# Folding the bias of the values into a bias row added in PSUM, and moving two pieces of VectorE's work to ScalarE, in a gated cross-attention with a mixture of experts

## The reference

```python
def attention(query, key, value, adj, mask):      # query = layernorm(x), key = value = ctx
    Q, K, V = heads(query @ Wq.T + bq), heads(key @ Wk.T + bk), heads(value @ Wv.T + bv)
    scores = Q @ K.T / sqrt(D) + adj              # per head, -inf where mask == 0
    out = merge(softmax(scores) @ V)
    return out @ Wo.T + bo

x = x + tanh(g_xattn) * attention(layernorm(x), ctx, ctx, adj, mask)
h = layernorm(x)
p = softmax(h @ gate_w.T);  e = argmax(p)         # one expert for each token
x = x + tanh(g_ffn) * p[e] * (relu(h @ w1[e] + b1[e]) @ w2[e] + b2[e])
```

## Time and profile before

| | us |
|---|---|
| three runs | 549.14, 551.38, 551.83 |
| median | 551.38 |
| span of the profiled execution, first to last instruction | 548.5 |
| PE busy in that span | 526.3 |
| DVE, ACT, POOL busy | 302.3, 309.1, 297.9 |

### The profile page before, as it was taken

The page is one execution under the profiler, slowest core; times in us unless marked ns, Lnnn a source line. Parts: engine busy times, 40 slices in busy tenths (PEclk is TensorE's granted clock), DMA queues, the critical chain, the costliest instruction groups (busy, mean ns, idle before and its releaser), DMA issues. The chain is left out here.

```text
span 548.5 us, 13306 instructions
## 1 busy us (share of the span) xinstructions
PE 526.3 (96%) x4123; PEld 405.1 (74%) x4124; DVE 302.3 (55%) x923; ACT 309.1 (56%) x678; POOL 297.9 (54%) x424
## 2 busy tenths in 40 slices
PE   8999999989999999999999999888999999999997
PEld 5577667667666667666676666658899999999996
DVE  2776587976677887668885878845340211111111
ACT  4366678665678665778675676664332333333322
POOL 5346566665567575468574556555244444443451
PEclk9999999999999999999999999999999999999999
DMA  8633625400405510204520057499136665555570
GB/s 288 206 110 132 192 65 183 149 31 6 150 21 192 166 50 1 79 10 153 180 85 1 11 184 250 147 362 320 59 103 218 211 205 196 178 187 184 189 210 1
DMA packets 51489, 77.67 MB, mean 142 GB/s; under 512 B 9945, under 2 KB 34601, under 8 KB 51305
## 3 DMA queue, kind: packets, MB, share of 16 engines
q1 hardware_dynamic: 46600, 67.72, 37.0%
q0 software_dynamic: 4192, 8.73, 5.0%
q10 hardware_dynamic: 640, 0.52, 0.3%
HBM read 52.76 MB, written 8.35 MB: 111 GB/s over the span
## 5 line engine op out<-in xcount | busy, mean ns | idle before, releaser
L1588 DVE CUSTOM_DVE_ANT_0 prob<-bank,adjm 128x512 f32<-128x512 f32 x256 | 172.3, 688 | 70.6 <-issue 39.9
L1229 ACT ACTIVATE pt<-bank 128x512 f32<-128x512 f32 x256 | 152.1, 596 | 87.7 <-PE bank L951 81.2
L682 POOL TENSOR_SCALAR prob<-prob,negmax 128x512 f32<-128x512 f32 x190 | 132.0, 698 | 117.6 <-DVE negmax L1588 113.4
L951 PE MATMUL bank<-ident,prob 128*128 128x128 f32 x1024 | 154.8, 274 | 2.2 <-POOL prob L682 1.3
L951 PEld LDWEIGHTS bank<-ident,prob 128*128 128x128 f32 x1024 | 124.2, 141 | 39.7 <-issue 13.7
L1299 ACT ACTIVATE adjm<-bank,colsm 128x128 f32<-128x128 f32 x184 | 52.6, 368 | 105.0 <-PE bank L1127 80.0
L940 PE MATMUL bank<-w2s 128*128 128x512 bf16 x256 | 97.5, 381 | 8.5 <-DVE negmax L1588 5.7
L963 PE MATMUL bank<-pt,vals 128*32 128x256 f32 x1024 | 68.3, 385 | 0.9 <-DVE vals L1386 0.5
L1127 PEld LDWEIGHTS bank<-xT,pt 128*128 128x128 f32 x576 | 67.1, 192 | 0.9
L1127 PE MATMUL bank<-xT,pt 128*128 128x128 f32 x576 | 67.2, 275 | 0.0
L1137 PE MATMUL bank<-w2s,adjm 128*128 x288 | 65.1, 379 | 0.0
(11 more groups left out here) (195 smaller groups left out, 624.4 us busy)
## 6 DMA issues: line engine op xcount, KB each, us to landing
pt<-in_L_ffn_w SPq DMA_DIRECT2D x19, 1024.0 KB
w2s<-parts SPq DMA_DIRECT2D x96, 128.0 KB
w2s<-in_L_ffn_w SPq DMA_DIRECT2D x8, 1024.0 KB
maski<-in_mask_Bx1xSxS_ik SPq DMA_DIRECT2D x4, 1024.0 KB, 5.6
w2s<-parts SPq DMA_DIRECT2D x56, 64.0 KB, 2.1
xres<-in_x SPq DMA_DIRECT2D x18, 128.0 KB
x_d<-rows SPq DMA_DIRECT2D x18, 128.0 KB
xn_d<-rows SPq DMA_DIRECT2D x18, 128.0 KB
```

The costliest lines, as they stand in the source:

```text
L682: po.tensor_scalar(prob[:, m], prob[:, m], -1.0, negmax[:, m:m + 1], ALU.mult, ALU.add).then_inc(s_shpool, 1)
L951: mm = pe.transpose(tr_bank[n % NTB][:, c * P:(c + 1) * P], prob[:, n % TILES % NB, c * P:(c + 1) * P], ident[:])
L1229: act.activation(pt[:, g % 2, :, j, q2 * P:(q2 + 1) * P], tr_bank[c % NTB][:].rearrange("p (c q) -> p c q", c=QT), ACT.Exp).then_inc(s_cac ...
L1588: ve.tensor_tensor_reduce(out=prob[:, m % NB], in0=sc_bank[m % NS][:], in1=adjm[:, qt], scale=-1.0, scalar=BIG, op0=ALU.add, op1=ALU.min, ...
```

## The change

1. **Values.** `bvb` is no longer added. ACT evicts a half of the values in one instruction of 128 x 512, in the step in which DVE had evicted it. DVE does nothing for it.
2. **Bias row.** In the setup PE transposes `bv` (step 4), ACT evicts it, PE multiplies it with Wo (step 8), and DVE adds `bob` and splits the sum into three bfloat16 rows that lie in partitions 0, 32 and 64 of `bias3` (`join_bias`, seven instructions). POOL fills `pick`, a 128 x 128 bfloat16 matrix with ones in rows 0, 32 and 64. The gate's weights are transposed one step later than before.
3. **Output.** Each `out` use starts with one more matmul, `pick` x `bias3`, which puts the bias into PSUM. DVE's L1416 goes, and L1418 reads PSUM. Its bank is set free one step later, at the head of `row_stats`.
4. **Normalised row.** DVE's L1447 goes. ACT writes the row in two instructions, mean minus x, then times 1 / sigma, in the same steps `ROW_STEPS`, behind the evictions of the step and ahead of L1255; the second waits for the first. The row has the other sign, and the two evictions of transposed rows (L1201 for `x2T`, L1293 for `xgT`) multiply by -1.
5. **Behind batch 3** ACT writes both rows behind the second slot's hidden layer, ahead of the eviction of the third slot's rows.

```diff
...
     PRO = ["Wq", "Wk", "small", "next x", "next x", "next ctx", "next ctx", "next q", "next k", "next q", "next k",
-           "Wv", "Wo", "gate"]
+           "Wv", "bv", "Wo", "bias", "gate"]
...
     MASK_STEPS, LATE_MASK_STEPS = {42: 0, 44: 1}, {13: 2, 15: 3}
-    WV_STEP, WO_STEP, GATE_STEP, FIRST_NORM_STEPS = 3, 6, 8, (2, 3, 4, 5)
+    WV_STEP, BV_STEP, WO_STEP, BIAS_STEP, GATE_STEP, FIRST_NORM_STEPS = 3, 4, 6, 8, 9, (2, 3, 4, 5)
...
         bob = sb("bob", [P, E])
+        bias3 = sb("bias3", [P, E], BF16)
+        pick = sb("pick", [P, P], BF16)
...
         x2T = sb("x2T", [P, 2, EC, P])
+        bvT = x2T[:, 0]
...
         t_x, t_out = ([sem(f"{n}{k}") for k in range(2)] for n in ("t_xres", "t_out"))
+        s_bias, t_centred, s_centred = sem("bias"), sem("t_centred"), sem("centred")
...
             po.memset(logit[:], 0.0).then_inc(t_ones, 1)
+            po.memset(pick[:], 0.0).then_inc(t_ones, 1)
+            po.wait_ge(t_ones, 3)
+            for r in range(3):
+                po.memset(pick[32 * r:32 * r + 1], 1.0).then_inc(t_ones, 1)
...
                     pe.wait_ge(t_atT, b * 4 + k + 1)
+                    if b == 0 and k == 0:
+                        pe.wait_ge(s_bias, 7)
+                        pe.wait_ge(t_ones, 6)
                     o = bank_free(b, i)
+                    pe.matmul(o[:, 0:E], pick[:], bias3[:], start=True, stop=False)
                     for c in range(EC):
-                        mm = pe.matmul(o[:, 0:E], atT[:, u, c], wT[:, 3, c], start=c == 0, stop=c == EC - 1)
+                        mm = pe.matmul(o[:, 0:E], atT[:, u, c], wT[:, 3, c], start=False, stop=c == EC - 1)
...
                     turn_w(2, setup_at("Wv"))
+                if n == BV_STEP:
+                    pe.wait_ge(s_bcast, 64)
+                    o = bank_free(0, setup_at("bv"))
+                    for c in range(EC):
+                        mm = pe.transpose(o[:, c * P:(c + 1) * P], bvb[:, c * P:(c + 1) * P], ident[:])
+                    mm.then_inc(s_m, 1)
...
                     turn_w(3, setup_at("Wo"))
+                if n == BIAS_STEP:
+                    for w in ("bv", "Wo"):
+                        pe.wait_ge(s_md[setup_at(w) % 2], free(0, setup_at(w)) + 1)
+                    o = bank_free(0, setup_at("bias"))
+                    for c in range(EC):
+                        mm = pe.matmul(o[:, 0:E], bvT[:, c], wT[:, 3, c], start=c == 0, stop=c == EC - 1)
+                    mm.then_inc(s_m, 1)
...
+            def values(b, i, h):
+                act.wait_ge(s_m, ready(b, i))
+                if b == 0 and h == 0:
+                    act.wait_ge(s_vinit, 2)
+                act.activation(vals[:, 2 * h:2 * h + 2, :, 0:D], sp_bank[i % 2][:].rearrange("p (t h d) -> p t h d", t=2, d=D),
+                               ACT.Copy).then_inc(s_v, 1)
+                act.wait_ge(s_v, b * 2 + h + 1)
+                act.sem_inc(s_md[i % 2], 1)
...
                 act.activation(dst[:, k % 2], sp_bank[i % 2][:, 0:E].rearrange("p (k q) -> p k q", k=EC),
-                               ACT.Copy).then_inc(done, 1)
+                               ACT.Copy, scale=1.0 if what == "turn" else -1.0).then_inc(done, 1)
...
                 act.sem_inc(s_md[i % 2], 1)
+            def norm_row(b, k):
+                u = k % 2
+                r = rows[:, u]
+                act.wait_ge(t_rstd, b * 4 + k + 1)
+                act.activation(r[:, E:2 * E], r[:, 0:E], ACT.Identity, scale=-1.0, bias=mv2[:, u, 0:1]).then_inc(t_centred, 1)
+                act.wait_ge(t_centred, b * 4 + k + 1)
+                act.activation(r[:, E:2 * E], r[:, E:2 * E], ACT.Copy, scale=rstd2[:, u:u + 1]).then_inc(t_row, 1)
...
                         next_use(b, i, what, k, b + 1)
+                    elif what == "values":
+                        values(b, i, k)
...
                         next_use(b, i, what, k, b + 1)
+                if n in ROW_STEPS[last]:
+                    norm_row(b, ROW_STEPS[last][n])
...
                     turned_w(2, setup_at("Wv"))
+                if n == BV_STEP:
+                    bv_use = setup_at("bv")
+                    act.wait_ge(s_m, ready(0, bv_use))
+                    act.activation(bvT.rearrange("p c q -> p (c q)"), sp_bank[bv_use % 2][:, 0:EC * P], ACT.Copy
+                                   ).then_inc(s_md[bv_use % 2], 1)
...
                 act.activation(xgT[:, u], xg_bank(u).rearrange("p (k q) -> p k q", k=EC),
-                               ACT.Copy).then_inc(f_xgT, 1)
+                               ACT.Copy, scale=-1.0).then_inc(f_xgT, 1)
...
             hidden(1, 1, e, 1)
+            norm_row(B, 0)
+            norm_row(B, 1)
...
                                         ).then_inc(s_md[i % 2], 1)
-            def values(b, i, h):
-                ve.wait_ge(s_m, ready(b, i))
-                for t in range(2):
-                    ins = ve.tensor_tensor(vals[:, 2 * h + t, :, 0:D],
-                                           sp_bank[i % 2][:, t * E:(t + 1) * E].rearrange("p (h d) -> p h d", d=D),
-                                           bvb[:].rearrange("p (h d) -> p h d", d=D), ALU.add)
-                    ins.then_inc((s_rest, s_v)[t], 1)
-                ve.wait_ge(s_v, b * 2 + h + 1)
-                ve.wait_ge(s_rest, b * 2 + h + 1)
-                ve.sem_inc(s_md[i % 2], 1)
...
                     ve.wait_ge(t_rowfree, b * 4 + k + 1)
-                    ve.tensor_tensor(r[:, 0:E], o[:, 0:E], bob[:], ALU.add).then_inc(s_md[i % 2], 1)
-                    ve.wait_ge(s_md[i % 2], free(b, i) + 1)
-                    ve.scalar_tensor_tensor(out=r[:, 0:E], in0=r[:, 0:E], scalar=tg[:, 0:1], in1=xres[:, u],
+                    ve.scalar_tensor_tensor(out=r[:, 0:E], in0=o[:, 0:E], scalar=tg[:, 0:1], in1=xres[:, u],
...
-            def row_stats(b, k):
+            def row_stats(b, i, k):
...
                 ve.wait_ge(t_x1, b * 4 + k + 1)
+                ve.sem_inc(s_md[i % 2], 1)
...
                 ve.bn_aggr(mv2[:, u], st2[:, u]).then_inc(t_mv, 1)
-            def norm_row(b, k):
-                u = k % 2
-                r = rows[:, u]
-                ve.wait_ge(t_rstd, b * 4 + k + 1)
-                ve.tensor_scalar(r[:, E:2 * E], r[:, 0:E], mv2[:, u, 0:1], rstd2[:, u:u + 1],
-                                 ALU.subtract, ALU.mult).then_inc(t_row, 1)
...
                 for i, what, k in at_step(uses, n - VE_AT):
-                    if what == "values":
-                        values(b, i, k)
-                    elif not what.startswith("next"):
+                    if what != "values" and not what.startswith("next"):
...
                     if what == "out":
-                        row_stats(b, k)
-                if n in ROW_STEPS[last]:
-                    norm_row(b, ROW_STEPS[last][n])
+                        row_stats(b, i, k)
...
                         norm_stats(1, t)
+            def join_bias(i):
+                ve.wait_ge(s_m, ready(0, i))
+                ve.wait_ge(s_bcast, 64)
+                ve.tensor_tensor(bob[:], bob[:], sp_bank[i % 2][:, 0:E], ALU.add).then_inc(s_bias, 1)
+                ve.wait_ge(s_bias, 1)
+                ve.sem_inc(s_md[i % 2], 1)
+                ve.tensor_copy(bias3[:], bob[:]).then_inc(s_bias, 1)
+                ve.wait_ge(s_bias, 2)
+                ve.tensor_tensor(bob[:], bob[:], bias3[:], ALU.subtract).then_inc(s_bias, 1)
+                ve.wait_ge(s_bias, 3)
+                ve.tensor_copy(bias3[32:64], bob[32:64]).then_inc(s_bias, 1)
+                ve.tensor_copy(bias3[64:P], bob[64:P]).then_inc(s_bias, 1)
+                ve.wait_ge(s_bias, 5)
+                ve.tensor_tensor(bob[64:P], bob[64:P], bias3[64:P], ALU.subtract).then_inc(s_bias, 1)
+                ve.wait_ge(s_bias, 6)
+                ve.tensor_copy(bias3[64:P], bob[64:P]).then_inc(s_bias, 1)
...
                     norm(1, FIRST_NORM_STEPS.index(n))
+                if n == BIAS_STEP:
+                    join_bias(setup_at("bias"))
...
             for k in range(2):
-                last_tail("out", k)
-                row_stats(B, k)
-            for k in range(2):
-                norm_row(B, k)
+                row_stats(B, last_tail("out", k), k)
...
             route_shift(B, [last_gate], B + 1, *RANKED[1])
...
```

## The result

Median of four runs 555.4 us (554.07 to 556.02) against 550.5 us (549.14 to 551.83) for the kernel before on the same chip. The ratio is 1.0086, with a 95% interval of 1.0058 to 1.0114: slower by 4.7 us, 3.2 to 6.3. The profiled execution took 555.86 us with a span of 554.1. The forecast was 555.1.

A forecast was written before the change was run, and what follows sets the result against it. PE was taken as the engine to watch, with DVE's relief paying only where PE waits for it. Terms 1.8 + 1.0 + 1.8 + 0.3 - 0.8 - 0.4 = +3.7 us gave 555.1 us, range 550.0 to 558.8.

The forecast's parts named there:

- PE's new work: 18 `out` uses, each with a `pick` matmul of 0.11 us; two in batch 3 counted at nothing; +1.8 us.
- the relief: DVE's shorter queue ahead of PE's waits: -0.8 us where batch 1 ends, -0.4 taken for batch 0.
- ACT's pair: Step 39, batches 0 to 2: two row instructions hold ACT 0.95 us, PE 0.6 us late at `gate`; +1.8.
- batch 3: Rows at steps 25 and 27: the chain to PE's wait at 317.34 gets longer through ACT; +0.3 us.
- D: Setup: `join_bias` longer, POOL's tile 10 late; 0.8 us for 3.5, 1.5 more for a fourth; 556.6, chance 0.10.
- E: Batch 3: ACT reaches a row before POOL's 1 / sigma, two exponentials behind it; 1.2 us, 556.3, chance 0.10.
- 3 x 0.45: High end of the range: dear ACT instructions, 1.4 us the pair, +0.45 in each of three batches.
- The setup: Bias product behind PE's DMA wait: four instructions of 0.216 and 0.1 for weight load, +1.0; `join_bias`, 2.5 us, hidden.
- the walk on POOL: Setup: POOL's subtraction of tile 10 ends near 46.0, PE wants it at 46.2; 0.2 us to spare.
- the gap of 0.38: End of batch 0: gap before DVE's tile at 110.62 may swallow the relief; between 0 and -0.8.
- Rival B: ACT has the room, so the row instructions of step 39 are swallowed too; 553.3 us, chance 0.20.
- C: DVE's queue is the true brake and all 8.1 us of PE's waits go; -5.0, 546.4 us, chance 0.14.

The follow-up runs named there:

- rows on DVE: Changed kernel with part 4 undone: DVE writes the normalised row again in one instruction, same steps; 554.5 us, ratio 1.0037.
- the values on DVE: Changed kernel with the values evicted by DVE, two copies of 128 x 256 for each half, without the bias; 557.3 us, ratio 1.0095.
- long join: Changed kernel with the last copy of `join_bias` made four times, same values; run once, "setup" 0.81 as in the changed kernel, no ratio.
- One pass alone: Kernel before, with rows of batches 0 to 2 written by ACT in one instruction and the masks' work moved; 552.3 us, ratio 0.9998.
- the rows on ACT alone: Kernel before with part 4 and nothing else: ACT writes the normalised row in two passes; 556.5 us, ratio 1.0071.
- the pair in step 38: Changed kernel with ACT's two instructions for row 1 moved from step 39 to step 38; ratio 1.0076.
- the mended kernel: Changed kernel; rows of batches 0 to 2 by ACT in one instruction, masks' work moved, rows of batch 3 and behind by DVE; 553.6 us, ratio 1.0022.

## Why the prediction was right, and where it was off

The direction and the mechanism held: PE's new work and ACT's lateness outweigh the relief. The total, +3.7 forecast, held as well; the terms as measured sum to 3.6 to 4.0, and the timed difference is 4.7 (3.2 to 6.3). But four of the terms were off in size and cancelled (PE's work by -0.7, ACT's pair by +0.7, batch 3 by +0.4 to +0.7, the relief by -0.3), so that their sum came out this close is luck. So is the time of 555.1 against 555.4: the difference was 1.0 us short, and a fourth run took the median of the kernel before from 551.4 to 550.5. The high end of the range, with D at 1.5, E at 1.2 and 3 x 0.45, adds up to 559.2 rather than 558.8, which changes nothing.

- **PE's new work, +1.8: too dear, 1.1.** The rule "work put on PE costs its full time unless it falls in front of a wait" missed that six of the pick matmuls fall into a gap that no wait shows, behind the products of 32 columns. Ten cost 0.11 (steps 33 and 56 of three batches, 20 and 22 of batch 3, two behind it), six 0.02, and two, in steps 52 and 55 of batch 3, lie ahead of the slots' wait: without pick that wait is 1.96 us instead of 1.78, though kernels alike have it at 1.3 to 1.9. (The 1.38 of "slots" without pick is no measure of it: a dip of the clock right behind the wait is in it.)
- **The setup, +1.0: 0.8 to 0.9** (against -0.12 where it is untouched). The bias product is the cost, 0.86 from its start at 36.79 to the scores at 37.65; the 0.1 more that was added for its weight load did not show. `join_bias` took 2.75 us, 2.5 forecast, hidden. The spare time behind it was more than the 0.2 given: a chain of 3.7 us still fits, with none left. What was wrong is the walk on POOL, which added the slot table's full length; in the kernel before, POOL's DMA at 41.18 follows an idle time of 1.40, in the changed one of 0.30.
- **ACT's pair, +1.8: mis-sized, 2.5.** Its mechanism is shown by undoing it (-0.84 a batch) and by doing it alone (+0.83 to 0.91). I had the shift of step 39 later by 0.7; it is 0.98 later. The pair doesn't fill the gap of 0.12 behind the eviction, it starts at 170.14 where the eviction ends at 170.02, and no idle time was left to take the rest. Of the 0.98 the next exponential made 0.15 good.
- **Batch 3, +0.3: mis-sized, 0.7 to 1.0** (1.25 where the bias add stays on DVE). The 0.49 of wait at 321.19, 0.31 more than before, is as reasoned. What was left out is that both pairs also delay exponentials there; and in step 27 ACT stands 0.25 us on POOL's 1 / sigma, ahead of 0.95 us of pair, which is a small piece of rival E.
- **Relief, -0.8 and -0.4: 1.5 in all in the changed kernel, 1.1 to 1.5 in those with the same rows and bias.** "End" holds the 0.11 of step 56's pick. Without it the end of batch 1 gave 0.74, of which the bias add alone gives 0.44 and the normalised row alone 0.33. The end of batch 0 gave 0.72, and there either alone gives all of it (0.77, 0.67), so my fear for the gap of 0.38 was wrong. As these columns differ by up to 0.4 between kernels alike, the split is rough. Behind batch 2: nothing.
- **The slots' DMA.** Relief at the end of batch 3 only lengthens PE's wait, as forecast. Costs from further ahead come through, since the DMAs are issued later by them: POOL's copy of the slots is 4.77 us later in the changed kernel, 1.14 with rows on DVE. PE's wait was 0.85 us before; after, and with rows on DVE:

```profile
366.21 0.19 POOL L663 COPY eidx<-slots 128x5 int32<-128x5 int32 x1 [3.24 <-DMA slots<-slot_d]
...
369.20 0.66 PE L963 MATMUL bank<-ident,prob 128*128 128x128 f32 x4 [1.78 <-POOL prob L690]
```
```profile
365.56 0.66 PE L963 MATMUL bank<-ident,prob 128*128 128x128 f32 x4 [2.46 <-POOL prob L690]
```

Rival B falls with the "mid" columns, C with the rows and the values on DVE (PE's waits for the maximum went from 5.7 to 4.6 us with 15 us less work on DVE), D with the long join. Of the signs named ahead, the stretch to step 44 grew by 0.84 instead of 0.6, the waits where batch 1 ends are gone, the slots' wait is longer, and the scores of step 14 come 0.88 later (46.38 against 44.96, less the 0.54 of "first").

Between the ledger (3.9 with the two picks behind batch 3) and the timed 4.7 there are 0.8 us, inside the interval. "Rest" is positive in all eleven traces, but much of that is a lucky profile of the kernel before: its span is 548.5 us, where the medians of 28, 26 and 17 later runs are 550.5, 550.1 and 550.4. One pass alone, as fast as the kernel before when timed, still has 1.44 us in "first", "slots" and "rest" together; the changed kernel has 1.93. What is left may lie in the dip of the clock below.

## What to carry to other kernels

Before work is moved to a less busy engine, read its timeline in the steps where it lands: ACT was busy for 60 of 86 us, and had 0.66 us of idle time where 1.9 arrived. Relief of an engine is worth at most the waits for it that it shortens, here 1.1 to 1.5 us for 15 us of work, and nothing close ahead of a wait for a DMA. Judge parts of under 1 us by distances between repeated instructions within traces, not by two spans.

## What the hardware showed that I had not expected

- **A dip of the clock behind a wait.** In six of the twelve profiled executions TensorE's granted clock fell to 0.50 (1.2 GHz) for some microseconds between 366 and 387 us, in four behind PE's wait at the slots and in two behind its wait for `region` some 15 us later. Windows of the changed kernel, then of the rows on ACT alone, which kept 1.00 (columns as in the earlier trace rows):

```profile
368.00:372.00 4.00, 2.67 (x16) 2.21 (x17) 0.00 (x0) 2.54 (x7) 3.13 (x5) 0.82 1.07 340
372.00:376.00 4.00, 4.00 (x35) 1.90 (x35) 0.51 (x3) 0.36 (x1) 0.81 (x1) 0.50 1.05 377
```
```profile
372.00:376.00 4.00, 3.87 (x51) 2.94 (x41) 1.42 (x9) 0.84 (x3) 0.97 (x2) 1.00 1.08 383
```

In it 32 products of weights and values took 3.64 us instead of 1.93. In the changed kernel most of that was covered: the wait for DVE's `region` that follows was 1.90 us before and 0.28 after. From the end of the slots' wait to the end of that wait it is 13.3 us, where the kernel before has 12.8 and the rows on ACT alone 12.9, so about 0.5 us was paid. With rows on DVE the wait for `region` stayed at 2.0, the same stretch is 15.2, and 2.4 us were paid, 1.9 of them in its 2.34 of "rest". The rows on ACT alone waited 0.97 us there, but the pair in step 38 and the long join waited 1.9 and 1.55 without a dip: what decides is open. The timed runs bear on how often it comes: the mean granted clock of an execution is 0.996 or less in 10 of 12 runs with rows on DVE and in 10 of 12 of the mended kernel, the two with the longest waits at the slots (2.46 and 2.05), against 5 of 28 and 4 of 17 of the kernel before beside them, which waited 0.85. Both also time above their ledger (2.1 and 1.1 us slower, with 0.60 and 0.40 in the columns from "setup" to "b3"). That the dip makes this difference is likely, not shown.

- **A matmul for nothing.** One bfloat16 matmul of 256 columns, put between sixteen products of 32 columns and a float32 one, cost 0.02 us instead of 0.11 (0.985 us to the next scores against 0.967, where step 33 has 0.975 against 0.866).
